# Time mix of a perceiver layer: the recurrence over the state written as a sum over lags, with the decays formed on GpSimd

## The reference, cut to what matters

```python
xx = shifted x - x
m = five small products of tanh((x + xx * tmx) @ maa_w1)
xw, xk, xv, xr, xg = x + xx * (tm_ + m[_])
r = xr @ Wr;  k = xk @ Wk;  v = xv @ Wv;  g = silu(xg @ Wg)
decay = exp(-exp(tdecay + tanh(xw @ td_w1) @ td_w2))
def step(S, inp):                       # one token; 16 heads of 8 channels
    r_t, k_t, v_t, d_t = inp
    kv = k_t[..., :, None] * v_t[..., None, :]
    y = einsum('bhi,bhij->bhj', r_t, S + u[None, :, :, None] * kv)
    return (d_t[..., None] * S + kv, y)
yn = per head: (y - mean) / sqrt(var + eps) * ln_w + ln_b
x = x + (yn * g) @ Wo
```

## Time and profile before

| | us |
|---|---|
| runs (3) | 662.43, 650.55, 657.82 |
| median | 657.82 |
| profiled execution | 651.66 |
| its span | 649.9 |

### The profile page before, as it was taken

How to read it: one execution, slowest core, us unless ns; L and a number is a source line. 1 busy time by engine, 2 the same in 40 slices (tenths; PEclk the granted TensorE clock), 3 DMA queues, 4 the chain that set the end, 5 groups by cost and what they waited for, 6 DMA issues and landing times. The chain is left out here.

```text
span 649.9 us, 14494 instructions
## 1 busy us (share of the span) xinstructions
PE 519.3 (80%) x4330; PEld 349.0 (54%) x4330; DVE 408.3 (63%) x784; ACT 342.2 (53%) x1022; POOL 381.8 (59%) x720
## 2 busy tenths in 40 slices
PE   3799999999999999359786996973375576967892
PEld 2467777777777777322222322331353465866792
DVE  7477887878778787642866838683748132333446
ACT  3688888888888887122307244243343233433440
POOL 4146666666666666274594876853554756656540
PEclk9989999999999999856889879998586779898997
DMA  9115562222222220000000000000110111111216
GB/s 219 48 53 170 162 169 83 73 78 68 80 73 73 74 64 26 2 0 0 1 1 0 0 2 1 0 1 0 32 33 2 35 39 45 46 38 45 42 34 194
DMA packets 57639, 34.15 MB, mean 53 GB/s; under 512 B 4298, under 2 KB 56356, under 8 KB 57604
## 3 DMA queue, kind: packets, MB, share of 16 engines
q1 hardware_dynamic: 55108, 28.60, 15.7%
q0 software_dynamic: 2496, 5.12, 2.9%
HBM read 29.05 MB, written 4.65 MB: 52 GB/s over the span
## 5 line engine op out<-in xcount | busy, mean ns | idle before, releaser
L571 ACT ACTIVATE probs<-psum,neg_max 128x289 f32<-128x289 f32 x256 | 125.8, 498 | 34.7 <-DVE neg_max L744 34.7
L744 DVE TENSOR_REDUCE neg_max<-psum 128x1 f32<-128x289 f32 (+1 forms) x192 | 95.4, 552 | 45.5 <-PE psum L677 45.5
L627 PE MATMUL psum<-ident,probs 128*128 128x128 f32 x512 | 83.0, 285 | 1.6 <-ACT probs L571 1.3
L627 PEld LDWEIGHTS psum<-ident,probs 128*128 128x128 f32 x512 | 59.4, 152 | 26.8 <-issue 24.7
L919 POOL TENSOR_TENSOR read<-recep,state 128x496 f32<-128x496 f32 x32 | 45.6, 1426 | 30.9 <-DVE state L1155 30.9
L1400 POOL DMA_INDIRECT y_rows<-x_sq,dest_row x39 | 38.3, 982 | 36.3 <-DVE x_sq L1719 29.4
L462 POOL TENSOR_TENSOR inv_spread<-quad_of,inv_sum 128x128 f32<-128x128 f32 x64 | 25.5, 398 | 56.5 <-DVE inv_sum L740 56.5
L677 PE MATMUL psum<-kT,q_heads 32*128 32x289 f32 x512 | 49.8, 458 | 0.8 <-ACT probs L571 0.8
L571 ACT ACTIVATION_READ_ACCUMULATOR probs<-psum,neg_max 128x1 f32 x256 | 50.5, 197 | 0.0
L1155 DVE TENSOR_TENSOR_SCAN state<-decay,kv 128x512 f32<-128x512 f32 x32 | 49.0, 1530 | 1.1
L1712 DVE TENSOR_TENSOR ex_hidden<-w_up,psum 128x352 f32<-128x352 f32 x39 | 20.3, 521 | 40.4 <-remote 19.9
(11 more groups left out here) (263 smaller groups left out, 1250.9 us busy)
## 6 DMA issues: line engine op xcount, KB each, us to landing
k_in<-in_ctx SPq DMA_DIRECT2D x64, 128.0 KB, 2.5
v_in<-in_ctx SPq DMA_DIRECT2D x64, 128.0 KB, 2.5
w_gate<-in_L_ffn_Wg SPq DMA_DIRECT2D x1, 1408.0 KB, 7.9
w_up<-in_L_ffn_Wu SPq DMA_DIRECT2D x1, 1408.0 KB, 7.0
x_res<-in_x SPq DMA_DIRECT2D x4, 256.0 KB, 3.7
v_own<-in_ctx SPq DMA_DIRECT2D x2, 512.0 KB, 7.2
w_down<-in_L_ffn_Wd SPq DMA_DIRECT2D x2, 512.0 KB, 5.0
x_rows<-x_cen SPq DMA_DIRECT2D x4, 256.0 KB, 2.3
```

Source lines behind the costliest of these rows:

```text
L571: last = nc.scalar.activation(probs_of(par, gr), bank[S_BANK[gr]][:, 0:KEYS], ACT.Exp, bias=neg_max[:, par, gr:gr + 1], accum_out=row_sum[ ...
L627: last = pe.transpose(bank[PT_BANK[h]][:, P * (2 * k + c):P * (2 * k + c) + P], probs_of(par, 2 * h + k)[:, P * c:P * c + P], ident[:])
L744: nc.vector.tensor_reduce(neg_max[:, par, start:end], psum[:, start:end, 0:KEYS], AX.X, ALU.max, negate=True).then_inc(s_max, 1)
```

## The change: what it does

y of token t is written as a sum over lags l of pairs of tokens t and t - l. For lag 0 the pair is r(t) u k(t). For lag l it is r(t) times the product of the decays between the tokens, times k(t - l). `sum` adds the pair over a head's channels by a product with `same_head`, `part` multiplies by v(t - l), and `y` adds the part into Y by a product with `centre`. All three are float32. Lag l has 16 (N - l) columns, since a sequence's first l tokens have no partner. The few words that name the change speak of 15 lags; the loops of the diff run over N, and N is 32 in this kernel, so the lags are 0 to 31.

- `decayed` (GpSimd): the receptance times one more decay, for lags 2 to 31, each from the one before it.
- `pair` (VectorE, both inputs in SBUF), `sum` (TensorE), `part` (VectorE, one input in PSUM), `y` (TensorE): once for each lag.
- In each slot of the list, `sum` is at its own lag, `y` three lags behind, `pair` two ahead, `part` one behind and `decayed` four ahead. `pair` and `part` have rings of 4 buffers, `decayed` of 3, and `sum` two banks.
- The mixing and the projections of block n + 1 and the norm of block n - 1 stand at fixed slots between the lags of block n. `mix`, `mix_part` and `mixed` have slots of their own. The projections have banks 0 and 1, which `hidden` uses as well.
- The weight splits come every third slot, all on the same engines as before.
- The scans, `kv`, `read`, the bonus steps, the split of the value and the constants `to_column` and `spread_value` go.

```diff
@@ -783,14 +783,10 @@
...
-            LAG = 2
+            RING = 4
+            AHEAD = 2
...
-            spread_value = scope.enter_context(nc.sbuf_tensor("spread_value", [P, D, C], F32R))
-            value_high = scope.enter_context(nc.sbuf_tensor("value_high", [P, BLK], F32R))
-            value_low = scope.enter_context(nc.sbuf_tensor("value_low", [P, BLK], F32R))
...
@@ -798,80 +794,90 @@
...
-            bonus_in = tile("bonus_in", [P, BLK])
-            bonus = tile("bonus", [P, 2, BLK])
-            kv = tile("kv", [P, 2, BLK])
-            state = tile("state", [P, LAG + 1, BLK])
-            read = tile("read", [P, LAG + 1, BLK])
...
+            value = tile("value", [P, 2, BLK])
+            decayed = tile("decayed", [P, 3, BLK])
+            pair = tile("pair", [P, RING, BLK])
+            part = tile("part", [P, RING, BLK])
...
+            PROJECT, SUM, Y, POST = (0, 1), (4, 5), bank[6], bank[7]
+            SEQ = "p (s n) -> p s n"
+
+
+
+            MIX_ORDER = (0, 3, 1, 2, 4)
+            PROJECT_ORDER = ("decay1", "r", "k", "decay2", "v", "g")
+            READ_BY = ("decay1", "k", "v", "r", "g")
+            LAGS = N * NB
...
+            order = [("shift", 0), ("hidden", 0)]
+            for f in MIX_ORDER:
+                order += [("mix", 0, f), ("mix_part", 0, f), ("mixed", 0, f)]
+                if f == 3:
+                    order.append(("project", 0, "decay1"))
+                if f == 1:
+                    order += [("project", 0, "r"), ("project", 0, "k")]
+                if f == 2:
+                    order += [("project", 0, "decay2"), ("project", 0, "v")]
+            order.append(("project", 0, "g"))
+            mix_slot = {6 + k: f for k, f in enumerate(MIX_ORDER)}
+            project_slot = {10: ("decay1",), 11: ("r",), 12: ("k", "decay2"), 13: ("v",), 14: ("g",)}
+            for step in range(-AHEAD - 1, LAGS + N):
+                n, slot = step // N, step % N
+                for kind, at in (("sum", step), ("y", step - 3), ("pair", step + AHEAD), ("part", step - 1), ("decayed", step + AHEAD + 2)):
+                    if 0 <= at < LAGS and (kind != "decayed" or at % N >= 2):
+                        order.append((kind, at // N, at % N))
+                if n >= 1:
+                    order += [(kind, n - 1) for kind, when in (("centre", 2), ("variance", 4), ("norm", 8), ("gated", 9), ("output", 11),
+                                                               ("residual", 12)) if slot == when]
+                if step >= 0 and step % 3 == 2 and step // 3 < len(splits):
+                    order.append(("split", step // 3))
+                if step >= 0 and n + 1 < NB:
+                    if slot == 2:
                         order.append(("shift", n + 1))
...
+                    if slot == 4:
+                        order.append(("hidden", n + 1))
+                    if slot in mix_slot:
+                        order.append(("mix", n + 1, mix_slot[slot]))
+                    if slot - 1 in mix_slot:
+                        order += [("mix_part", n + 1, mix_slot[slot - 1]), ("mixed", n + 1, mix_slot[slot - 1])]
+                    order += [("project", n + 1, k) for k in project_slot.get(slot, ())]
...
+                        if n:
+                            pool.wait_ge(s_project, project_no(n - 1, READ_BY[f]) + 1)
+                        g.tensor_tensor(mixed[:, f, :], mix_part[:, m % 2, :],
                                         ln_T[:, BLK * n:BLK * n + BLK], ALU.add).then_inc(s_mixed, 1)
-                    elif s == ("project", n, "v"):
-                        pool.wait_ge(s_value, n + 1)
-                        if n:
-                            pool.wait_ge(s_prod, prod_no[("state", n - 1, D - 1)] + 1)
-                        g.tensor_tensor(value_low[:], value[:], value_high[:].bitcast(F32), ALU.subtract).then_inc(s_value_low, 1)
-                    elif s == ("project", n, "decay2"):
-
-                        pool.wait_ge(s_decay, n + 1)
-                        g.memset(decay[:, par].rearrange(SEQ, n=N)[:, :, 0:1], 0.0).then_inc(s_decay_cut, 1)
-                    elif s[0] == "state":
-                        q = D * n + s[2]
...
-                        g.tensor_tensor(read[:, q % (LAG + 1)].rearrange(SEQ, n=N)[:, :, 1:N],
-                                        recep[:, par].rearrange(SEQ, n=N)[:, :, 1:N],
-                                        state[:, q % (LAG + 1)].rearrange(SEQ, n=N)[:, :, 0:N - 1], ALU.mult).then_inc(s_read, 1)
...
+                    elif s[0] == "decayed":
+                        lag = s[2]
+                        if lag == 2:
+                            pool.wait_ge(s_recep, n + 1)
+                            pool.wait_ge(s_decay, n + 1)
+                        else:
+                            pool.wait_ge(s_decayed, decayed_no(n, lag))
+                        if lag >= 5:
+                            pool.wait_ge(s_pair, lag_no(n, lag - 3) + 1)
+                        elif n:
+                            pool.wait_ge(s_pair, lag_no(n, 0))
+                        near = recep[:, par] if lag == 2 else decayed[:, (lag - 1) % 3]
+                        g.tensor_tensor(decayed[:, lag % 3].rearrange(SEQ, n=N)[:, :, lag:N],
+                                        near.rearrange(SEQ, n=N)[:, :, lag:N],
+                                        decay[:, par].rearrange(SEQ, n=N)[:, :, 1:N - lag + 1], ALU.mult).then_inc(s_decayed, 1)
+                    elif s[0] == "split":
+                        pool.wait_ge(s_w_high, s[1] + 1)
+                        exact, high, low = weight_parts(*splits[s[1]])
+                        g.tensor_tensor(low, exact, high.bitcast(F32), ALU.subtract).then_inc(s_w_low, 1)
...
                     elif s[0] == "project":
+                        if s[2] in ("decay1", "r"):
+                            pe.wait_ge(s_mix, 5 * n + 1)
+                            pe.wait_ge(s_hidden_out, n + 1)
+                        elif s[2] == "k":
+                            pe.wait_ge(s_dhidden, n + 1)
+                        elif s[2] == "decay2":
+                            pe.wait_ge(s_recep, n + 1)
+                        elif s[2] == "v":
+                            pe.wait_ge(s_key, n + 1)
+                        else:
+                            pe.wait_ge(s_dexp, n + 1)
+                        out_ = project_bank(n, s[2])
...
-                    elif s[0] == "bonus":
-                        pe.wait_ge(s_bonus_in, n + 1)
-                        product(s, same_head[:], bonus_in[:])
-                    elif s[0] == "state":
...
+                    elif s[0] == "sum":
+                        lag = s[2]
+                        q = lag_no(n, lag)
+                        pe.wait_ge(s_pair, q + 1)
+                        if q >= 2:
+                            pe.wait_ge(s_part, q - 1)
+                        some = SPB * (N - lag)
+                        pe.matmul(bank[SUM[q % 2]][:, 0:some], same_head[:], pair[:, q % RING, 0:some],
+                                  start=True, stop=True).then_inc(s_sum, 1)
                     elif s[0] == "y":
-                        j = s[2]
-                        q = D * n + j
-                        pe.wait_ge(s_tocolumn, 1)
-                        pe.wait_ge(s_read, q + 1)
-                        if j == 0 and n:
-                            pe.wait_ge(s_y_sq, n)
-                        pe.matmul(Y, to_column[:, j, :], read[:, q % (LAG + 1)], start=(j == 0), stop=(j == D - 1)).then_inc(s_y, 1)
-                    elif s[0] == "add_bonus":
-                        pe.wait_ge(s_bonus, n + 1)
-                        pe.matmul(Y, centre[:], bonus[:, par], start=False, stop=False)
+                        lag = s[2]
+                        if lag == 0:
+                            pe.wait_ge(s_centre, 1)
+                            if n:
+                                pe.wait_ge(s_y_sq, n)
+                        pe.wait_ge(s_part, lag_no(n, lag) + 1)
+                        pe.matmul(Y.rearrange(SEQ, n=N)[:, :, lag:N], centre[:],
+                                  part[:, lag_no(n, lag) % RING, 0:SPB * (N - lag)].rearrange(SEQ, n=N - lag),
+                                  start=(lag == 0), stop=(lag == N - 1)).then_inc(s_y, 1)
...
+                    elif s[0] == "pair":
+                        lag = s[2]
+                        if lag == 0:
+                            v.wait_ge(s_recep, n + 1)
+                            v.wait_ge(s_key, n + 1)
+                        elif lag >= 2:
+                            v.wait_ge(s_decayed, decayed_no(n, lag) + 1)
+                        q = lag_no(n, lag)
+                        if q >= RING:
+                            v.wait_ge(s_sum, q - RING + 1)
+                        if lag == 0:
+                            nc.vector.scalar_tensor_tensor(pair[:, q % RING], recep[:, par], params[:, PAR_BONUS:PAR_BONUS + 1],
```

(66 more changed lines are left out.)

149 lines of the change are left out of this document (42 added, 107 removed).

## The result

The changed kernel takes 721.12 us (median of 4 runs, 719.66 to 721.81), against 657.0 for the kernel before (4 runs on the same chip, 650.55 to 662.43): a ratio of 1.101, 95% interval 1.096 to 1.106. It is slower by 10%. The forecast was 694, its range 669 to 726.

A forecast was written before the change was run, and what follows sets the result against it. TensorE (157 us) and the access shared by VectorE and GpSimd (154) were taken to bound the loop at 180; with start 21 and end 12, 213 against 172.2, 41 more, gave 692.7, forecast 694, range 669 to 726.

The forecast's parts named there:

- the two limits: State loop: TensorE with 157 us and the access shared by VectorE and GpSimd with 154, lying differently within a block.
- the sum: Time-mix stage: start 21, loop 180 and end 12 make 213 us against 172.2, giving 692.7 for the profiled execution.
- some 210: Sign of being right: the time-mix stage of the changed kernel is some 210 us long.
- rival 3: Loop: narrow slots cost 0.9 us, not 0.5, or clock stays at 0.87 or below; time 715 to 730; chance 0.26.
- The 180 itself: Loop: larger of both loads over groups of four slots, 175 us at clock 1.00, 189 at 0.90; taken as 180.
- The step said: Stage start: 2 us less, 21, from interleaving project with mix; bounds 5 less and 1 more.
- "Five mix ... at 0.86": TensorE, per block: six project, five mix and two hidden products at 0.86 us each, 11.2 together.
- VectorE's 28 a block: VectorE in the loop: pair and part 21.4 us a block, 28 with mix_part, shift, norm and residual.
- Rival 1: Loop: order slides perfectly with TensorE the bound, or access is shared more kindly; loop 157 to 163, time 673; chance 0.17.
- The step I thought most at risk: Narrow lags: a slot costs 0.5 us; slots near 1 us, every engine idle between waits, would show it wrong.
- The 30 us that early projection was to save: Block boundaries: projecting the next block in slots 10 to 14 removes 7 to 12 us at each of three, about 30.

## Why the prediction was right and wrong

**Right: the direction, the two limits and the size of the arithmetic.** The replaced recurrence was cheaper than 135,168 column passes. TensorE is busy all through slots 4 to 15. Slots 8 to 15 keep their length when GpSimd is relieved, and 8 to 11 go from 11.8 to 9.6 us when `sum` is halved: there it is the bound. In slots 28 to 3 it idles. There the sum had 3.4 us for slots 28 to 31 and 8.8 for 0 to 3, from `decayed` and `pair` one behind the other; measured are 3.9 to 4.3, and 8.5 to 9.7 in blocks 0 to 2 (5.8 in block 3, which has no `shift`). `pair` is stretched and `part` is not. TensorE's part of block 3, which projects nothing, was 31.4; it was busy 33.2. The end kept its chain and its length.

**The misses added up.** The profiled execution took 720.8 us where the sum had 692.7: 28 more. Of these 11.3 are the start (32.3 for 21), 12.4 the loop and the end together (204.4 for 192) and 4.5 outside the stage, where the sum had no change. The stage took 236.8 us, not "some 210". That the time still lies in the range is partly luck: the range reached to 726 because rival 3 had a chance of 0.26, and rival 3 isn't what happened. The 180 itself was a choice between 175 at a clock of 1.00 and 189 at 0.90. A slip that changes little: block 0's share of TensorE is 40.9 by its own terms, not 40.2.

**Wrong: the start, 32.3 for 21.** The step said that the interleaved order costs at most 1 us, "since TensorE's same 28 passes stand there". Of the 28 two belong to the first state; the 26 of mixing and projections are the same. But the order wasn't weighed, nor was the clock: at 2 us a product each projection put between two `mix` products delays the next `mixed`, g's stands before the first `sum`, and the whole start ran at 0.50 instead of 0.61. Undone, the start is 21.85. This is the largest single miss, some 10 us.

**Mis-sized: the loop, 193.5 for 180** (181.1 with the cut used here). In slots 4 to 7 the sum had 10.3 us from TensorE; measured are 12.0, 13.1 and 11.3. Two terms account for most of the 12.4. "Five mix ... at 0.86" took the price of a full-row product for one of 32 rows: about 5 us by the run with full rows. `decay1` and `decay2` are spaced 1.01 and 1.05 in the trace (0.15 and 0.19 too much each) and weren't tried. `shift` was worked into VectorE's 28 a block at 1.4 us (the figure is in the expectation above); it takes 3.3 there, and the move is worth 4.1 net. The clock has a share in both: slots 4 to 7 of block 1 took 1.8 us more at 0.87 than those of block 2 at 1.00, behind a stretch in which TensorE had idled. The remaining 3 us I can't assign.

**The rivals.** Rival 1 (sharing kinder, 673) fell: even with the `decayed` steps off GpSimd TensorE is busy 175 us, at a granted clock of 0.99. The time lies in rival 3's interval, but not by its mechanism. The narrow slots at the end of block 3 (`sum` alone is shown; a `y` stands between two of them):

```profile
510.42 0.36 PE L1060 MATMUL psum<-pair,same_head 128*128 128x96 f32 x2
510.89 0.34 PE L1060 MATMUL psum<-pair,same_head 128*128 128x80 f32 x2
511.33 0.33 PE L1060 MATMUL psum<-pair,same_head 128*128 128x64 f32 x2
```

A slot is 0.44 to 0.47 us, 0.11 a pass, not 0.9, and the loop's clock is 0.95, not 0.87. The step I thought most at risk held. The 30 us that early projection was to save are not visible as a gain: its work sits in slots where TensorE is full. In the old loop, where TensorE had room, a version of it with v and g left behind the states was worth 4 to 5 us of 655.

## What to carry to other kernels

Before a recurrence is replaced by a sum over lags, add the column passes that the sum needs, and compare them with what the recurrence leaves idle. Here 193.5 us of loop took the place of 138.0, and no reordering of it came below 187. Shortening the products of a bound engine helps only where that engine is the bound, and only as far as its clock holds. At the start of a stage, where TensorE runs at its lower level, put the products that feed a chain first and those that nobody awaits last. Price each product by a row of its own shape, in the company it will have.

## What the runs showed of the hardware

- The granted clock fell as passes were taken away: 0.95 in the changed loop, 0.86 with one pass for `sum`, 0.66 with one pass for both, where TensorE was busy 140 of 180 us. Halving the second product bought nothing.
- The granted clock fell after TensorE had idled at a block start, and the next slots paid: 13.1 us at 0.87 in block 1, 11.3 at 1.00 for the same slots of block 2.
- `pair` of 480 columns took 1177 ns beside GpSimd's `decayed` and 649 with those steps on VectorE. `part`, with one input in PSUM, took 646 and 649.
- A product of 32 rows (1.06) or 64 rows (1.05, `decay2` at 354.54) among fp32 products of 128 rows is farther from the next start than the 0.86 us of a `w_time` product (351.57 to 352.43); so is `decay1`, which has 128 rows and 64 output columns (1.01). For 32 rows, filling them removed it.
- A VectorE operation of 16 columns takes 1.07 us beside a GpSimd operation at a block's start, where 0.17 had been seen undisturbed, and `pair` of 16 columns 354 ns in the mean. With the `decayed` steps on VectorE both take 0.17 to 0.18 us: the rest was waiting, not data.
